# One read tree of a gated delta-rule kernel: its first addition done by an accumulating DMA, the rest half an iteration later, and another order of loads in the first block

## The reference

```python
xn  = layernorm(x)
out = x + attn(xn) + experts(xn)

# attn: gated delta rule, 16 heads of 16, for every token t in order
S  = S * g[t]                          # state, 16x16 a head
S += b[t] * outer(k[t], v[t] - k[t] @ S)
o[t] = q[t] @ S                        # the "read" of the state
# then x1 = xn + o @ Wo + bo, and x1 + gelu(layernorm(x1) @ w1 + b1) @ w2 + b2

# experts: router softmax, top 8 of 64 experts, at most 128 rows each;
# gather an expert's rows, silu(x@wg) * (x@wu) @ wd, scatter-add to the tokens; one shared expert
```

## Time and profile before

| | us |
|---|---|
| median of three runs (lowest, highest) | 1885.25 (1883.35, 1887.22) |
| the profiled execution's own time | 1889.32 |
| its span, first to last instruction | 1887.6 |
| busy VectorE | 1692.2 (90%) |
| busy GpSimd | 1591.6 (84%) |
| busy TensorE, matmul | 1417.8 (75%) |
| busy ScalarE | 813.4 (43%) |
| DMA engines' mean busy share, queue of SyncE | 34.3% |
| DMA engines' mean busy share, queue of GpSimd | 7.3% |

### The profile page before, as it was taken

The page is one execution under the profiler, slowest core; times in us unless marked ns, Lnnn a source line. Parts: engine busy times, 40 slices in busy tenths (PEclk is TensorE's granted clock), DMA queues, the critical chain, the costliest instruction groups (busy, mean ns, idle before and its releaser), DMA issues. The chain is left out here.

```text
span 1887.6 us, 31473 instructions
## 1 busy us (share of the span) xinstructions
PE 1417.8 (75%) x8846; PEld 1235.2 (65%) x8846; DVE 1692.2 (90%) x4987; ACT 813.4 (43%) x2548; POOL 1591.6 (84%) x1353
## 2 busy tenths in 40 slices
PE   6777777877764677566565658898888989988869
PEld 5666666766653566455554647777777877777657
DVE  3599999999999999899977987999899999999980
ACT  4534444545444544345432245444544444434313
POOL 5279999899998889788887788998899899999861
PEclk9978778878875788787877679998999999899878
DMA  8574334533346666856658421242123311111110
GB/s 187 146 179 114 75 99 118 139 83 97 95 124 152 166 149 159 214 116 152 163 135 229 88 54 50 68 131 83 56 58 109 90 53 53 65 50 58 42 50 18
DMA packets 337169, 201.24 MB, mean 107 GB/s; under 512 B 208226, under 2 KB 327716, under 8 KB 336996
## 3 DMA queue, kind: packets, MB, share of 16 engines
q1 hardware_dynamic: 318724, 168.43, 34.3%
q0 software_dynamic: 15616, 30.55, 7.3%
q10 hardware_dynamic: 2656, 0.26, 0.1%
HBM read 127.58 MB, written 71.60 MB: 106 GB/s over the span
## 5 line engine op out<-in xcount | busy, mean ns | idle before, releaser
L823 POOL TENSOR_TENSOR rp<-S,qs 128x2048 f32<-128x2048 f32 x113 | 521.2, 4612 | 44.6 <-DVE S L1144 30.5
L1144 DVE SCALAR_TENSOR_TENSOR S<-S,gwin,bank 128x256 f32<-128x256 f32 x1024 | 481.0, 470 | 0.3
L1134 DVE TENSOR_REDUCE nu<-vwin 128x16 f32<-128x272 f32 x1024 | 435.9, 426 | 0.3
L1138 DVE TENSOR_TENSOR bank<-nu,bank 128x256 f32<-128x256 f32 x1024 | 428.6, 419 | 0.6
L1129 DVE TENSOR_TENSOR vwin<-S,bank 128x256 f32<-128x256 f32 x1024 | 419.7, 410 | 0.3 <-DVE nu L1134 0.2
L831 POOL TENSOR_TENSOR r<-rp 128x1024 f32<-128x1024 f32 x113 | 273.5, 2420 | 7.0
L1792 PE MATMUL bank<-region 128*128 128x128 f32 x2048 | 278.0, 294 | 0.0
L1792 PEld LDWEIGHTS bank<-region 128*128 128x128 f32 x2048 | 262.2, 207 | 18.3 <-issue 17.8
L1672 PE MATMUL bank<-xaT,wqkvg 128*128 128x128 f32 (+1 forms) x1792 | 237.8, 285 | 11.9 <-ACT xaT L1326 8.5
L1803 PE MATMUL bank<-region 128*128 128x256 f32 x1024 | 234.8, 383 | 0.0
L1672 PEld LDWEIGHTS bank<-xaT,wqkvg 128*128 128x128 f32 (+1 forms) x1792 | 212.4, 187 | 26.4 <-ACT xaT L1326 12.6
(11 more groups left out here) (170 smaller groups left out, 2275.0 us busy)
## 6 DMA issues: line engine op xcount, KB each, us to landing
qkv_d<-stg SPq DMA_DIRECT2D x192, 128.0 KB, 3.0
region<-in_L_ffn_w_gate SPq DMA_DIRECT2D x64, 192.0 KB, 4.5
region<-in_L_ffn_w_up SPq DMA_DIRECT2D x64, 192.0 KB, 4.9
region<-in_L_ffn_w_down SPq DMA_DIRECT2D x64, 192.0 KB, 5.9
region<-in_L_attn_x SPq DMA_DIRECT2D x16, 512.0 KB, 7.2
region<-in_L_attn_x SPq DMA_DIRECT2D x32, 256.0 KB, 4.4
xw_d<-region SPq DMA_DIRECT2D x32, 256.0 KB, 3.4
acc_d<-region SPq DMA_DIRECT2D x32, 256.0 KB, 4.2
```

The source lines that it names most:

```text
L823: g.tensor_tensor(rp[:, :, :].rearrange("p (a v) d -> p a v d", v=DH), S[h][:, lo:lo + HS].rearrange("p t s (v d) -> p (t s) v d", v=DH), ...
L1134: m[G] = mark(v.tensor_reduce(nu[:, G], products_of(I, s, G)[1], AX.X, ALU.add))
L1138: m[G] = mark(v.tensor_tensor(outer[G].rearrange("p (v d) -> p v d", v=DH), nu[:, G].unsqueeze(2).to_broadcast([P, DH, DH]), key(L, s, G), ...
L1144: ins = v.scalar_tensor_tensor(S[h][:, s, G], earlier(h, s, G), gwin[:, I // NB2 & 1, G, 1, t:t + 1], outer[G], ALU.mult, ALU.subtract)
```

## The change

- `r1` goes. `rp` and `rx` become the two entries of `halves`; each is laid out as two planes of 128x1024: the product writes elements 0 to 7 of each value to plane 0 and 8 to 15 to plane 1.
- `fold` is the product and then, once it has finished, a DMA issued by GpSimd that adds plane 1 to plane 0 within SBUF (512 KB, rows of 4 KB). It replaces L831.
- `tree` is the rest of the additions, from plane 0, once the fold has landed (`fold_done`).
- The order: half 0's fold, then what stood between product and tree (scatter 0, or place 2), then `behind(I - 1)`: the tree of the previous iteration's half 1 and, behind j = 7, the block's store. Then scatter 1 (or place 1), half 1 (`fold`, or `products` as before), scatter 2, and only then half 0's tree. In the iterations that end an output part (I = 59 and 63) the tree and the store are done at once.
- VectorE's `read_sum` also waits for the earlier block's store.
- First block: GpSimd issues for each group keys, gates, values; the queries of both groups come last. Gates, values and queries have semaphores of their own. VectorE scales only the first 8 tokens' values of both groups and starts; GpSimd scales the other 56 tokens' of both, and VectorE waits for them at I = 1.

The core of the diff:

```diff
+        halves = [b[:, :, :].rearrange("p a d -> p (a d)").rearrange("p (c a d) -> p c a d", c=2, d=DH // 2) for b in (rp, rx)]
...
+            def fold(I, h, half):
...
+                g.tensor_tensor(
+                    halves[half].rearrange("p c (a v) d -> p a v c d", v=DH),
+                    S[h][:, lo:lo + HS].rearrange("p t s (v c d) -> p (t s) v c d", v=DH, c=2),
+                    qs[h][:, lo:lo + HS].rearrange("p t s (c d) -> p (t s) c d", c=2).unsqueeze(2).to_broadcast([P, HS * 2, DH, 2, DH // 2]),
+                    ALU.mult).then_inc(prod_done, 1)
+                pool.wait_ge(prod_done, I * 2 + (3 + half))
+                g.dma_start(halves[half][:, 0], halves[half][:, 1], accum_op=ALU.add).then_inc(fold_done[half], 16)
+                folds[half] += 1
+
+            def tree(I, half):
+                lo, r = half * HS, halves[half][:, 0]
+                pool.wait_ge(fold_done[half], folds[half] * 16)
+                link(g.tensor_tensor(r[:, :, 0:4], r[:, :, 0:4], r[:, :, 4:8], ALU.add))
+                link(g.tensor_tensor(r[:, :, 0:2], r[:, :, 0:2], r[:, :, 2:4], ALU.add))
...
+            def behind(I):
+                if I < 0 or I + 1 in PARTS_END:
+                    return
+                if not summed(I):
+                    tree(I, 1)
+                if I % NB2 == NB2 - 1:
+                    store_block(I)
...
+                fold(I, h, 0)
                 if X0 <= I < X1:
-                    reads(I, h, 0, j, lambda: scatter(n * RT, 0, h))
+                    scatter(n * RT, 0, h)
+                    behind(I - 1)
                     scatter(n * RT + 1, 1, h)
                     if summed(I):
                         products(I, h)
                         scatter(n * RT + 2, 2, h)
                     else:
-                        reads(I, h, 1, j, rows_ahead)
+                        fold(I, h, 1)
+                        scatter(n * RT + 2, 2, h)
+                        if I + 2 < X1:
+                            gather(n + 2, n % 2)
+                    tree(I, 0)
                 else:
-                    reads(I, h, 0, j, lambda: back_roots(I, 2))
+                    back_roots(I, 2)
+                    behind(I - 1)
...
                     if I + 1 < NI:
-                        reads(I, h, 1, j)
+                        fold(I, h, 1)
+                    tree(I, 0)
...
+        def first_keys_load(queue, s):
+            queue.dma_start(win[1][:, 0, s], qkv_ld[0, 1, s]).then_inc(first_key[s], 16)
+            for w in range(2):
+                queue.dma_start(gwin[:, 0, s, w], gat_ld[0, s, w]).then_inc(first_gate[s], 16)
+            queue.dma_start(vwin[:, 0, s, :, DH:DH + BLK], qkv_ld[0, 2, s]).then_inc(first_val[s], 16)
...
-                dve.wait_ge(*window_in(0, 1))
-                vw = vwin[:, 0, 1, :, DH:DH + BLK]
-                v.tensor_tensor(vw, vw, rk[:, 1, :].unsqueeze(1).to_broadcast([P, DH, BLK]), ALU.mult).then_inc(vals_ready, 1)
+                for s in range(2):
+                    dve.wait_ge(*values_in(0, s))
+                    vw = vwin[:, 0, s, :, DH:DH + ST]
+                    mark(v.tensor_tensor(vw, vw, rk[:, s, 0:ST].unsqueeze(1).to_broadcast([P, DH, ST]), ALU.mult))
```

More of the change, by code:

```diff
@@ L167, in sums_before @@
     return sum(summed(i) for i in range(I))
+PARTS_END = tuple(SEG[1] + (n + 1) * PT // ST for n in range(PARTS))
 NYW = 6
@@ L362, in layer @@
         first_key = [sem(f"first_key{s}") for s in range(2)]; first_win = [sem(f"first_win{s}") for s in range(2)]
+        first_gate = [sem(f"first_gate{s}") for s in range(2)]; first_val = [sem(f"first_val{s}") for s in range(2)]
         first_st = [[sem(f"first_st{s}{i}") for i in range(BUF)] for s in range(2)]
@@ L813, in scale_values @@
             def scale_values(k, s):
-                vw = vwin[:, k & 1, s, :, DH:DH + BLK]
-                g.tensor_tensor(vw, vw, rk[:, s, :].unsqueeze(1).to_broadcast([P, DH, BLK]), ALU.mult).then_inc(vals_ready, 1)
-            def reads(I, h, half, j, mid_work=None):
+                lo = 0 if k else ST
+                vw = vwin[:, k & 1, s, :, DH + lo:DH + BLK]
+                g.tensor_tensor(vw, vw, rk[:, s, lo:BLK].unsqueeze(1).to_broadcast([P, DH, BLK - lo]), ALU.mult).then_inc(vals_ready, 1)
+            folds = [0, 0]
+            def fold(I, h, half):
                 lo = half * HS
@@ L870, in _ @@
             pool.wait_ge(sv_ready, 1)
-            scale_values(0, 0)
+            for s in range(2):
+                pool.wait_ge(*values_in(0, s))
+                scale_values(0, s)
             def residual(I):
@@ L966, in _ @@
                         route_factors(I + 3)
+                if I + 1 in PARTS_END:
+                    if I + 1 < NI:
+                        tree(I, 1)
+                    else:
+                        pool.wait_ge(last_read, 2)
+                    store_block(I)
                 if h == 1:
                     relink()
-                if I == NI - 1:
-                    pool.wait_ge(last_read, 2)
-                if j == NB2 - 1 and I < SEG[1]:
-                    pool.wait_ge(x_sums, 2 * sums_before(I))
-                    for s in range(2):
-                        g.dma_start(o_st[I // NB2, s], oblk[:, s].rearrange("p v t -> p (v t)")).then_inc(o_stored, 16)
-                if I >= SEG[1] and (I + 1) * ST % PT == 0:
-                    n = (I - SEG[1]) * ST // PT
-                    for s in range(2):
-                        g.dma_start(ol_st[n, s], oblk_l[:, n, s].rearrange("p v t -> p (v t)")).then_inc(o_stored, 16)
             for i in range(LAST, NT):
@@ L1265, in _ @@
             for k in range(NBLK):
-                dve.wait_ge(vals_ready, (k + 1) * 3)
+                if k:
+                    dve.wait_ge(vals_ready, (k + 1) * 3)
                 for s in range(2):
                     dve.wait_ge(*keys_in(k, s))
-                for s in range(2):
-                    dve.wait_ge(*window_in(k, s))
+                    dve.wait_ge(*values_in(k, s))
+                    dve.wait_ge(*gates_in(k, s))
                 stage_factors(k)
```

51 lines of the change are left out of this document (32 added, 19 removed).

## The result

| | before | after |
|---|---|---|
| median of 4 runs each (lowest, highest), us | 1886.13 (1883.35, 1887.22) | 1960.86 (1956.63, 1966.73) |
| ratio, 95% interval | | 1.040 (1.0376 to 1.0423) |
| profiled execution: its time, its span | 1889.32, 1887.6 | 1956.63, 1954.9 |

The forecast was 1872 with a range of 1845 to 1898. The time is 75 us above before and 63 us outside the range.

What follows compares the result with a forecast made beforehand. VectorE was taken as the bound everywhere, with GpSimd second and almost without slack. Back -22, expert +13, router 0, first block -4 and tail 0 gave -13 us on the runs' median 1885.25: 1872 us, range 1845 to 1898.

Steps and rivals of the forecast that it cites:

- landing is hidden: Back stretch: folds land before their trees need them, so GpSimd's relief shortens VectorE's waits: -22 us (0 to -33).
- The tests named for it: Back stretch: ScalarE's 162 us for GpSimd falls by some 40, VectorE's L1113 waits from 33.5 to about 11.
- Price of the fold on GpSimd: Each read: gap 0.64 plus issue 0.59 us replaces a 2.42 us addition, saving 1.2 us (0.2 to 1.8).
- Expert stretch: Scatters with nothing between them lengthen GpSimd's iteration; VectorE loses 2.1 us in each of 6: +13 us (-8 to +42).
- x: Expert stretch: delay of scatter 0 by the fold ahead of it in the queue, taken as 1 us (0 to 6).
- First block: Start of the kernel: earlier gates and smaller scaling let VectorE start about 8 us earlier, worth -4 us (0 to -8).
- the 2.3 us of room: First block: slack of VectorE's first expert product at I = 1 before it must wait for ScalarE's result.
- Router stretch: While the router runs: no wait for GpSimd to remove and folds hidden, so 0 us (-3 to +3).
- tail: Last store: 5 us later but still in cover of VectorE's sum, 0 us, or +3 if landing is slow.
- Rival 2: Expert and back stretches: the fold is free for the scatters, the back stretch gains all its 33: 1845 us; chance 0.17.
- rival 3: Expert stretch: scatter 1 waits for the fold, with a delay of 4 us: 1902 us; chance 0.18.
- rival 4: Back stretch: relief does not arrive, through a costly accumulating issue or TensorE as the limit: 1889 us; chance 0.20.

Runs made afterwards that it cites:

- e5: Changed kernel with GpSimd adding instead of the fold's DMA, and half 0's tree between scatters 0 and 1 in the expert iterations: 1895.64 us, ratio 1.0052.
- e10: As e5, but with the fold by DMA from iteration 35 on, both halves: 1933.84 us, ratio 1.0268.
- e4: Changed kernel with a fold that adds only an eighth, in rows of 512 B (leaves out part of the computation): 1878.83 us, ratio 0.9966.
- e3: Changed kernel with the fold's DMA a plain copy instead of an accumulate (leaves out the first addition): 1899.67 us, ratio 1.0065.
- e11: As e10, but only half 0's fold is by DMA and GpSimd adds for half 1: 1914.31 us, ratio 1.0137.
- e1: Changed kernel with the fold's DMA replaced by a GpSimd addition, order and first block as changed: 1926.08 us, ratio 1.0211.
- e2: Kernel before the change with the first block's part of the change alone: 1883.91 us, ratio 0.9984.
- e7: Changed kernel with the back stretch's output stores issued by ScalarE instead of SyncE: 1954.24 us, ratio 1.036.

## Why the prediction was wrong

**The step that failed: "landing is hidden" in the back stretch, -22 us.** It was measured at about +52. The step asked whether the fold is in time for its own tree, and there it was right: 4.9 us of waits in 55 folds. It put the time that a fold takes of the DMA engines at nothing and gave no reason (their share was 0.23), and never asked what else crosses them. Some 12 of the 52 us are there without any fold, with the new order alone (e5, unexplained); with the folds of this stretch alone it is 49 (e10). Each fold takes them for 2.7 us, twice what GpSimd pays for it, at places tied to GpSimd's order and not to the loads. The `o_d` loads of SyncE come in rows of 64 tokens, 256 B, are issued one behind the other, and the tile buffers are four deep, so a late load comes back as a late `back_x1` and a later next load. That chain I read from the timeline and the waits; that the folds' occupancy of the engines is the cause is shown by e4, e3 and the changed kernel, equal but for it (-4.7, +9.9 and +52.1 us from I = 36 to 63), and by e10 and e11, where it goes with their number. Both the issues and the data are later: a tile's three loads take 13.0 us from the first issue to the landing instead of 11.2 (mean of tiles 8 to 55), about half of the difference in the issues and half behind them. SyncE's own 256 B packets take an engine 18 ns in the median before and after, so they wait longer rather than move more slowly. By what mechanism SyncE's issues get longer is open.

**The tests named for it.** ScalarE's wait for GpSimd was to fall by 40 from 162: it fell by 93. VectorE's waits at L1113 were to fall from 33.5 to 11, and to be wrong if above 25: 44.0. The first was the mechanism, the second its worth: the wait removed was replaced by one for TensorE's loads. With so few bytes that the loads stay in time (e4) the back stretch does gain, -4.7 us up to I = 63 and -14.0 up to I = 57. That is less than 22 us, and part of e4's 47 us lies in the expert stretch (its offset at 36 is -6.3, e1's +22.1). So even with the engines free the gain was over-sized.

**Price of the fold on GpSimd: 1.23 us, saved 1.2.** Right: 0.30 of gap and 0.92 of issue are 1.22, in other parts (0.64 and 0.59 had been taken). The accumulating form costs 0.3 us more to issue than the plain one (0.92 against e3's 0.61), and the gap is 0.3. The product's new shape costs nothing: 4.67 and 4.56 us in the mean against 4.61.

**Expert stretch: +13 (-8 to +42).** Measured +24, within the bounds, and more than the 13. Right were the arithmetic of the regular iteration (x there 0.8 against 1) and the sign. Too small was the number of iterations: VectorE was to lose only in the 6 in which it had waited. GpSimd lags in nearly all of them. Its third scatter, after less before, goes from -4.9 us in iteration 19 to +13.5 in 23, with scatter distances up to 9.05, and from +7.9 in 24 to +22.5 in 31. VectorE doesn't lose this iteration by iteration, since it does not need GpSimd in each. It loses 13.3 us in iteration 23 and 5.2 in 31, the two ahead of a change of block, where GpSimd also scales the next block's values: 18.5 of the 24 us in two iterations. In e1, with no fold by DMA, the same place costs 16.0. Nor is the loss where I looked in the waits: those for the second product grew from 30.9 to only 34.1 us, not to 44, and the rest is at other places that are as late:

```profile
DVE oblk L1238 <- POOL rx L901: 34.1, 9, 6.9
DVE bank L1118 <- POOL vwin L840: 15.9, 2, 8.0
DVE hg_s L1125 <- ACT sgu L1479: 8.8, 7, 2.3
```

The last two were 5.7 and 0.7 us before; the two waits of 8.0 for the scaled values are those of iterations 23 and 31. A wait row tells where an engine stood, not how often a slower partner will be felt.

**First block: -4 (0 to -8).** Right by sum, -3.4 by the trace and -3 by e2's ratio, less so by parts. The roots on ScalarE start at 61.84 us instead of 66.17 (forecast: near 61). The two scalings were to take 0.9 us and took 4.3:

```profile
65.61 4.29 DVE L1277 TENSOR_TENSOR vwin<-vwin,rk 128x128 f32<-128x128 f32 x2
```

```profile
65.61 4.14 POOL L840 TENSOR_TENSOR vwin<-vwin,rk 128x896 f32<-128x896 f32 x2 [6.16 <-DVEq L1273]
```

The row that the 0.9 was scaled from was not VectorE's own time. In the kernel before GpSimd scales the other group from the same start as VectorE's 3.44 us:

```profile
69.95 2.36 POOL L816 TENSOR_TENSOR vwin<-vwin,rk 128x1024 f32<-128x1024 f32 x1 [10.52 <-DVEq L1216]
```

VectorE's product of 128x1024 ended 1.08 us after GpSimd's, and each of the two of 128x128 now ends 0.15 us after one of GpSimd's. What was made eight times smaller was the 1.08 us, not the 3.44.

So the recurrence starts 3.4 us earlier and not 8, and the 2.3 us of room at the first expert product was not what limited it: VectorE's first L1125 is at 106.2 us and not near 103. The sum was right by two errors that met, which is luck.

**Router stretch 0, tail 0.** -1.8 us from I = 0 to 20. From I = 63 to the end of the span -3.3 (67.3 - 70.6). The first holds; the tail came out 3.3 us better than 0, and what did that is open. One wait was not foreseen: the first fold of half 1 waits 15.6 us for the store of zeros out of the same buffer; it costs VectorE nothing that can be seen.

**The rivals.** Rival 2 fell with the 5.3 us and more between scatters, rival 3 because x is 0.8 in the regular iterations and about 1.9 in the mean of the 13, below the 2.1 from which it was to decide (in two iterations the distance did pass its 8 us), rival 4 because the relief arrived. The slower rivals put the price on GpSimd's queue or on the scatters; none put it on the loads of another engine's queue. The bound "nothing" at the upper end of the back stretch had no reason behind it but TensorE's own busy time, and it cut the range off where the result lay.

## What to carry to other kernels

A DMA that replaces an addition is not paid where it is issued. Before moving bytes onto the DMA engines, take their time a transfer from a queue row (share x span / count; here twice a copy's for an accumulate), multiply by the transfers, and ask which engine's loads have short rows, a serial issuer and few buffers: theirs is the wait that grew here, at a mean share of only 0.42. When the partner's period exceeds the bound engine's, charge every iteration, not only those in which a wait stands today; the lag adds up unseen and is paid where the bound engine next needs the partner, here at a change of block. And test a new order by itself: here it cost 39 us without any fold by DMA.

## What the runs showed of the hardware

- An accumulating DMA within SBUF of 512 KB in rows of 4 KB took all 16 engines for 2.7 us, the plain copy of the same bytes for 1.35 us; a 4 KB packet takes one engine 328 and 159 ns in the median. GpSimd issued them in 0.92 and 0.61 us.
- The duration of SyncE's issues depends on what other queues move: one form of store was issued in 0.57 us in the median before, 0.93 in e4, 1.64 in e3 and 2.58 in the changed kernel.
- VectorE's product with two inputs in SBUF ended 1.08 us (128x1024) and 0.15 us (128x128, twice) after a GpSimd product of 128x1024 or 128x896 that had started at the same time or up to 0.1 us before; so 128x128 took 2.2 us. The Trainium skill ("SBUF — State Buffer", section "SBUF: two separate sides") says that VectorE with two SBUF inputs and a GpSimd instruction that reads SBUF share one port pair, as a lock held for a whole instruction, with the other blocked; these ends agree with that. No run here has VectorE's product without GpSimd beside it.
- Output stores taken off SyncE's queue did not bring its loads earlier: from the last issue to the landing it took 8.1 us instead of 5.9 (e7 and the changed kernel).
